# Cross attention of a decoder layer: normalised x written to PSUM, split into fp16 pairs and transposed by DMA, projected in fp16 with a scaled W, in a new instruction order

## What is computed

```python
x = x + attn(layernorm(x))            # one head of 128, scores, softmax, w_o
x = x + xattn(layernorm(x), ctx_1024, mask)
x = x + ffn(layernorm(x))             # ternary weights, 8-bit activations, silu

def xattn(x, y, y_mask):
    x_proj = relu(einsum('bih,oh->bio', x, W) + b)
    y_proj = relu(einsum('bjh,oh->bjo', y, W) + b)
    scores = einsum('bih,bjh->bij', x_proj, y_proj)
    scores = where(y_mask[:, None, :], -inf, scores)
    return einsum('bij,bjh->bih', softmax(scores), y)
```

## Time and profile before

| | us |
|---|---|
| median of 3 runs | 364.05 |
| lowest, highest | 363.34, 364.35 |
| the profiled execution | 364.81 |
| span of its core in the profile | 363.0 |

### The profile page before, as it was taken

The page is one execution under the profiler, slowest core; times in us unless marked ns, Lnnn a source line. Parts: engine busy times, 40 slices in busy tenths (PEclk is TensorE's granted clock), DMA queues, the critical chain, the costliest instruction groups (busy, mean ns, idle before and its releaser), DMA issues.

```text
span 363.0 us, 7155 instructions
## 1 busy us (share of the span) xinstructions
PE 350.5 (97%) x1980; PEld 258.2 (71%) x1980; DVE 323.2 (89%) x932; ACT 311.9 (86%) x583; POOL 293.6 (81%) x421
## 2 busy tenths in 40 slices
PE   8999799999999999999999999999999999999986
PEld 7477578867876767776686776877687667668545
DVE  3689969968899889997899899999999999899994
ACT  3597998999999968999689976899789978898985
POOL 1475859658999998889868998799987897996776
DMA  7984761462046552398456492739564533213353
GB/s 283 419 204 150 173 178 30 124 141 85 17 111 137 118 158 60 79 204 163 88 137 140 66 226 82 159 95 190 116 70 122 114 98 73 46 29 74 93 112 117
DMA packets 84695, 46.09 MB, mean 127 GB/s; under 512 B 76208, under 2 KB 77872, under 8 KB 84272
## 3 DMA queue, kind: packets, MB, share of 16 engines
q1 hardware_dynamic: 84656, 45.64, 52.1%
HBM read 23.07 MB, written 4.21 MB: 75 GB/s over the span
## 4 chain that ended last, share of the span: by engine, by line
PE 52%; DVE 22%; issue 9%; ACT 6%; POOL 6%; DMA 5%; SPq 0%; DVEq 0%; ACTq 0%; POOLq 0%
PE b_bank L1133 6%; PE b_bank L1135 6%; PE b_bank L1134 6%; PE a_bank L1133 3%; PE a_bank L1135 3%; PE a_bank L1134 3%; PE g_bank L1350 3%; PE d_bank L1370 3%; PE u_bank L1350 3%; DMA x_all<-in_x 2%; PE b_bank L1278 2%; DVE h_max L1646 2%; DMA out<-x_all 2%; DVE b_pT_lo L1589 2%; DVE c_work L1619 1%
## 5 line engine op out<-in xcount | busy, mean ns | idle before, releaser
L755 POOL TENSOR_TENSOR c_work<-c_work 128x512 f32<-128x512 f32 x48 | 61.7, 1290 | 5.9 <-DVE c_work L1619 3.6
L1021 ACT ACTIVATE c_work<-g_bank,c_tanh_scale 128x512 f32<-128x512 f32 x52 | 36.2, 696 | 4.5 <-PE g_bank L1350 3.9
L802 POOL TENSOR_SCALAR c_work<-c_work,h_q 128x1024 f32<-128x1024 f32 x28 | 31.5, 1124 | 8.6 <-DVE h_q L1653 8.6
L1133 PE MATMUL b_bank<-ctx_hi,b_pT_hi 128*128 128x256 f32 x128 | 38.2, 299 | 0.1
L1619 DVE SCALAR_TENSOR_TENSOR c_work<-c_work,g_bank 128x512 f32<-128x512 f32 x50 | 33.9, 677 | 3.2 <-ACT c_work L1021 2.8
L1134 PE MATMUL b_bank<-ctx_lo,b_pT_hi 128*128 128x256 f32 x128 | 36.1, 282 | 0.0
L1135 PE MATMUL b_bank<-ctx_hi,b_pT_lo 128*128 128x256 f32 x128 | 36.1, 282 | 0.0
L1350 PE MATMUL g_bank<-gateT,xqT 128*128 128x512 bf16 x112 | 33.6, 382 | 1.3 <-ACT xqT L996 0.7
L1350 PE MATMUL u_bank<-upT,xqT 128*128 128x512 bf16 x112 | 33.6, 381 | 0.3 <-DVE c_work L1614 0.2
L1646 DVE TENSOR_REDUCE h_max<-c_work 128x1 f32<-128x1024 f32 x26 | 31.4, 1209 | 1.0 <-POOL c_work L755 1.0
L1370 PE MATMUL d_bank<-downT,c_half 128*128 128x256 bf16 x240 | 31.2, 273 | 0.2 <-ACT a_xT_raw L1048 0.2
(11 more groups left out here) (375 smaller groups left out, 1237.3 us busy)
## 6 DMA issues: line engine op xcount, KB each, us to landing
ctx_raw<-in_ctx SPq DMA_DIRECT2D x8, 512.0 KB, 4.3
a_xT_raw<-in_x_t SPq DMA_DIRECT2D x7, 512.0 KB, 5.0
ctxT_raw<-in_ctx_t SPq DMA_DIRECT2D x7, 512.0 KB, 4.0
x_all<-in_x SPq DMA_DIRECT2D x7, 512.0 KB, 3.9
out<-x_all SPq DMA_DIRECT2D x7, 512.0 KB, 3.0
r_bc<-r_rows SPq DMA_DIRECT2D x7, 256.0 KB, 4.0
c_work<-in_w_gate SPq DMA_DIRECT2D x1, 1024.0 KB, 9.6
c_work<-in_w_up SPq DMA_DIRECT2D x1, 1024.0 KB, 11.6
```

The source lines that it names most:

```text
L755: pool.tensor_tensor(h[:, t % 2, half * HALF:(half + 1) * HALF], th[:, j % 2, :], up[:, j % 2, :], ALU.mult).then_inc(hs, 1)
L802: pool.tensor_scalar(h_tile(t, n), h_tile(t, n), h_q[:, t:t + 1], ROUND if n < LAST else ROUND_F16, ALU.mult, ALU.add).then_inc(h_rounds, 1)
L1021: act.activation(gate_tile(j, n), gu_bank("g", j, n), ACT.Silu if (n, j) in SILU else ACT.Tanh, scale=c_tanh_scale[:, j // 2:j // 2 + 1]). ...
L1133: pe.matmul(dst, l_hi, r_hi, start=first, stop=False)
```

## The change

1. `b_xn`, `b_T_hi`, `b_T_lo` and the steps XT0 and XT1 on PE are gone. ACT writes the normalised x of a half (two token tiles, 128x512) into a PSUM bank (`b_norm`): `b0`, `b1` for batch 0, `e` for all others. ACT rounds that bank to fp16 (`xn_hi`), DVE subtracts for the low part (`xn_lo`), and SP transposes the pair with one DMA for each half (`transpose_xn`), 128x1024 fp16 each. In the lists these are ACT `B.norm`, ACT and DVE `B.XT0`, `B.XT1`, SP `S.xnT0`, `S.xnT1`.
2. XP0 and XP1 multiply fp16 pairs. W is scaled into the fp16 range once (`w16_max`, a sum over partitions on PE `W.ws`, `w16_scale`, `w16_hi`, `w16_lo`), and the relu takes the scale back (`scale=w16_back`).
3. The `e` bank is shared by YP0, YP1, X0, X1 of all later batches in an order of its own (`E_STEPS`), with the waits that go with it. All five lists are written anew.

```diff
 def b_step(step, n):  # PE
-    if step[:2] == "XT":
...
-            mm = pe.transpose(dst[:, s * P:(s + 1) * P], b_xn[:, s, t * P:(t + 1) * P], ident[:, :])
-    elif step[:2] == "XP":
...
-        pe.wait_ge(b_los, b_lo_rank("XT1", n))
...
+    if step[:2] == "XP":
         if n > 0:
             pe.wait_ge(*o_read(2 + t, n - 1))
...
+        for half in range(2):
+            pe.wait_ge(xn16_loaded[half], 16 * n + 16)
+        xnT = xn16T[:, :, :, :].rearrange("p h (l t c) q -> p h l t c q", l=2, t=2)
         for c in range(DC):
-            mm = product3(dst[:, :], wt_hi[...], wt_lo[...], b_T_hi[:, c, :], b_T_lo[:, c, :], c == 0, c == DC - 1)
+            mm = product3(dst[:, :], w16_hi[...], w16_lo[...], xnT[:, :, 0, :, c, :], xnT[:, :, 1, :, c, :], c == 0, c == DC - 1)
+def b_norm(half, n):  # ACT
+    act.wait_ge(b_shifts, 2 * n + half + 1)
+    before = A_BEFORE[f"X{half}", n]          # who had the bank before
...
+    for i in range(2):
+        t = 2 * half + i
+        last = act.activation(a_bank(f"X{half}", n)[:, i * D:(i + 1) * D], x_tile(n, t), ACT.Identity,
+                              scale=b_rstd[:, t:t + 1], bias=b_shift[:, t:t + 1])
+def xn_hi(half, n):  # ACT
+    act.wait_ge(b_xns, 2 * n + half + 1)
+    if n > 0:
+        act.wait_ge(xn16_loaded[half], 16 * n)
+    act.activation(xn16[:, half, 0:S], a_bank(f"X{half}", n)[:, :], ACT.Copy).then_inc(x_his, 1)
+def xn_lo(half, n):  # DVE
+    dve.wait_ge(x_his, 2 * n + half + 1)
+    dve.tensor_tensor(xn16[:, half, S:2 * S], a_bank(f"X{half}", n)[:, :], xn16[:, half, 0:S], ALU.subtract).then_inc(x_los, 1)
+def transpose_xn(half, n):  # SP
+    sp.wait_ge(x_los, 2 * n + half + 1)
+    if n > 0:
+        sp.wait_ge(xn16_loaded[half], 16 * n)
+        sp.wait_ge(b_filled, b_rank("XP1", n - 1))
+    sp.dma_start(xn16T[:, half], xn16[:, half, :], transpose=True).then_inc(xn16_loaded[half], 16)
+def scale_W(part):  # DVE
...
+        dve.tensor_reduce(w16_max[:, :], W_raw, AX.X, ALU.max, apply_absolute_value=True).then_inc(w16_maxed, 1)
...
+        dve.tensor_scalar(w16_back[:, :], b1_bank[:, 0:1], 1.0e-30, 1.0 / F16_TOP, ALU.max, ALU.mult).then_inc(w16_steps, 1)
...
+        dve.reciprocal(w16_scale[:, :], w16_back[:, :]).then_inc(w16_steps, 1)
...
+        dve.scalar_tensor_tensor(w16_lo[...], W_raw, w16_scale[:, :], w16_hi[...], ALU.mult, ALU.subtract).then_inc(w16_split, 1)
-A_STEPS = "Q K YP0 V VT S0 S1 P0 S2 YP1 P1 S3 P2 P3 H Y0 Y1"
+A_STEPS = "Q K V VT S0 S1 P0 S2 P1 S3 P2 P3 H Y0 Y1"
+X_FIRST = "X0/0 X1/0"
+E_STEPS = """YP0/2 YP1/2 YP0/3 X0/1 X1/1 X0/2 YP1/3 X1/2 YP0/4 YP1/4 X0/3 X1/3 YP0/5 YP1/5 X0/4 X1/4 YP0/6 X0/5
```

More of the change, by code:

```diff
@@ L44 @@
 NEXT_BANKS = ["a0", "a1"]
-E_BANK = "e"
+X_FIRST_BANKS = ["b0", "b1"]
 def a_heir(step, n):
@@ L63, in a_tables @@
     later = [key for key in later if key not in following]
-    turns = [itertools.chain(FRONT_BANKS, itertools.cycle(FRONT_TURN)), iter(SECOND_BANKS), itertools.cycle(NEXT_BANKS)]
+    parts = [front, following, keys(X_FIRST.split()), later, keys(E_STEPS.split())]
+    turns = [itertools.chain(FRONT_BANKS, itertools.cycle(FRONT_TURN)), iter(SECOND_BANKS), iter(X_FIRST_BANKS),
+             itertools.cycle(NEXT_BANKS), itertools.repeat("e")]
     place, banks, before, last = {}, {}, {}, {}
-    for part, turn in zip((front, following, later), turns):
+    for part, turn in zip(parts, turns):
         for step, n in part:
@@ L70, in a_tables @@
             else:
-                if step[:2] != "YP":
+                if step[0] not in "YX" or step[:2] in ("Y0", "Y1"):
                     place[step, n] = len(place)
-                banks[step, n] = E_BANK if part is later and step[:2] == "YP" else next(turn)
+                banks[step, n] = next(turn)
                 before[step, n] = last.get(banks[step, n])
@@ L79 @@
 A_PLACE, A_BANK, A_BEFORE, A_LAST = a_tables()
-B_STEPS = ["XT0", "XT1", "XP0", "XP1", "S0", "S1", "P0", "S2", "P1", "O0", "S3", "P2", "O1", "P3", "O2", "O3"]
+B_STEPS = ["XP0", "XP1", "S0", "S1", "P0", "S2", "P1", "O0", "S3", "P2", "O1", "P3", "O2", "O3"]
 WARM_UP = 6
@@ L85 @@
 DVE_WHOLE = [("K", 0), ("P1", 0), ("P3", 0)]
-B_LO = ["XT0", "XT1", "P0", "P1", "P2", "P3"]
+B_LO = ["P0", "P1", "P2", "P3"]
 NBL = len(B_LO)
@@ L102 @@
 PE_ORDER = """
[L103 to L117, removed]
@@ L118 @@
-    C.g4/3 B.P2/4 B.O1/4 A.H/5 C.g5/3 E.YP0/6 A.Y0/5 A.Y1/5 B.P3/4 C.u5/3 A.Q/6 B.O2/4 C.g6/3 C.u6/3 A.K/6 A.V/6
-    B.O3/4 C.g7/3 B.XT0/5 B.XT1/5 C.u7/3 A.S0/6 C.DN0/3 B.XP0/5 B.XP1/5 C.u0/4 C.g0/4 E.YP1/6 A.S1/6 A.S2/6
-    C.DN1/3 C.u1/4 C.g1/4 B.S0/5 B.S1/5 C.DN2/3 C.g2/4 A.S3/6 C.DN3/3 C.u2/4 B.P0/5 B.S2/5 B.P1/5 C.u3/4 C.g3/4
-    B.O0/5 B.S3/5 C.g4/4 C.u4/4 B.P2/5 B.O1/5 A.H/6 C.u5/4 B.P3/5 C.g5/4 C.u6/4 A.Y0/6 A.Y1/6 B.O2/5 A.Q/7 A.K/7
-    B.O3/5 A.V/7 A.S0/7 C.g6/4 B.XT0/6 B.XT1/6 C.DN0/4 C.u7/4 C.g7/4 A.S1/7 B.XP0/6 B.XP1/6 C.g0/5 E.YP0/7
@@ L1079, in step @@
                     if stream == "B":
[L1080 to L1084 removed]
+                        b_norm(half, n)
                     else:
@@ L1394, in step @@
                     mm.then_inc(v_sums, 1)
+                elif name == "ws":
+                    pe.wait_ge(w16_maxed, 1)
+                    pe.wait_ge(v_steps, 1)
+                    pe.matmul(b1_bank[:, 0:1], ones[:, :], w16_max[:, :], start=True, stop=True).then_inc(w16_summed, 1)
                 elif name == "total":
+                    pe.wait_ge(w16_steps, 1)
                     pe.wait_ge(v_steps, 1)
```

346 lines of the change are left out of this document (193 added, 153 removed).

## The result

The change makes the kernel slower: 374.72 us median of 4 runs (373.77 to 378.69) against 364.02 (363.34 to 364.35), ratio 1.0317 with an interval of 1.0239 to 1.0395. The prediction said 359.7 us and faster, with a range of 355.0 to 365.0. The profiled execution took 378.69 us with a span of 376.6, against 364.81 and 363.0; it is the slowest of the four, so what is read from its trace explains 13.6 us of span and not the 10.7 us between the medians.

The account below looks back on a forecast made before the run. PE was taken as the bound by a little, DVE next. 363.0 - 8.8 (PE's work) + 0.2 (sum for W's scale) + 2.4 (batch 0) + 1.9 (DVE) = 358.7 us span, 359.7 us predicted; range 355.0 to 365.0.

Parts of the forecast that it names:

- What bounds the kernel: Whole kernel, chiefly 100 to 340 us: PE is full and the bound by a little, DVE next at 94.2%.
- PE's own work, -8.8 us: PE: 7.3 us from removed transposes of x and 1.5 us from shorter fp16 matmuls of XP0 and XP1.
- The fall of PE's busy time by 17 us: Sign on the profile page: PE's busy time down by some 17 us of records, 8.7 of XT among them.
- ACT and DVE at nothing: Normalisations, roundings and subtractions of x: same counts with fp16 out, 0.3 us more over two engines, taken at nothing.
- Scaled W, hidden: Preparation of W: 2 us of DVE in steps of about 0.7 us or less, hidden in idle time before 40 us.
- Batch 0, +2.4 us, XP0 at 50.6: Batch 0: DMA path not covered, 1.17 us of transposes not gained and XP0 1.2 us later, +2.4 us.
- the last part: Closing list of signs: prediction wrong if batch 0's delay grows along the pipeline, or POOL or ACT turns out next.
- The DMA wait, covered in batches 1 to 7: Before XP0: other PE work covers the transposes' latency; tightest batch 5 some 0.6 us short, bounds 0 to 1.5 a batch.
- DVE gives back 1.9: 100 to 340 us: DVE holds 96%, not the needed 96.8%, +1.9 us, bounds 0 and +6.4.
- Rival 2 (SP's queue), 372 us: SP: transposes of x held 5.8 us behind others stop PE 1.8 us or more a batch, 12.6 in all; chance 0.14.
- Rival 1 (PE's work brings nothing): 100 to 340 us: DVE at 94.2% is the bound, so PE's 6.4 us do not come; 364 us, chance 0.15.

Follow-up runs that it names:

- x_oneXT: Kernel before, with one PE transpose instead of four in each of XT0 and XT1 of batches 1 to 7: 365.52 us, ratio 1.0027.
- x_lessACT: Kernel before, batches 1 to 7: one PE transpose of four, DVE's subtraction and ACT's rounding of x over 64 of 512 columns: 364.28 us, ratio 1.0000.
- x_front: Changed kernel with two entries of DVE's list moved, A.ag1/1 earlier and W.wl/0 later: 373.34 us, ratio 1.0277.
- x_nowait: Changed kernel, XP0 and XP1 of batches 1 to 7 multiply a fixed buffer without waiting for the transposes, which are still issued: 371.93 us, ratio 1.0216.
- x_free: Changed kernel, batches 1 to 7: XP does not wait for the transposes, and these take a constant source without waiting for x: 369.49 us, ratio 1.0180.
- x_late: Kernel before, with XP0 of each batch waiting for one added small store of 128x4 numbers on SP: 389.54 us, ratio 1.0656.
- x_bslot: Kernel before without the loads of x of batches 4 to 7, which use the output of four batches before: 364.06 us, ratio 0.9994.
- x_slot: Changed kernel without the loads of x of batches 4 to 7, which use the output of four batches before: 372.23 us, ratio 1.0238.

## Why the prediction was wrong, step by step

- **What bounds the kernel: wrong, and the root of the error.** "PE is not waiting, it is full" was read from distances inside groups of matmuls; it is true there and says nothing of what happens when a group gets shorter. PE's list then reaches the next step earlier and waits for other streams. `x_oneXT` to `x_lessACT` measure it: 4.6 us on PE, 6 on DVE, 4 on ACT, sum zero.
- **PE's own work, -8.8 us: right** (8.5 by the starts; fp16 matmuls of XP at 0.214 us for 0.217), but it is no gain. The fall of PE's busy time by 17 us that I named as a sign was mis-sized: it was 4.6. The rows give only 8.7 us of XT and some 2 us of XP (records of 0.38 for 0.40 us), and the rest has no working.
- **ACT and DVE at nothing: right for what was counted, and one term was left out.** The normalisation, the rounding and the subtraction cost 0.564, 0.595 and 0.684 us. The relu with the scale costs 0.79 us for 0.705, 2.6 us of ACT. What it costs in time no run measures.
- **Scaled W, hidden: wrong.** `w_lo` took 2.22 us where I said 0.7 or less, and stood on the chain to XP0 of batch 0, in DVE's list ahead of the second shift. Away from a long POOL instruction it takes 0.78 us (last section), so the price was nearly right and the place was wrong. `x_front`, which moves it, is 1.4 us faster by the medians, inside the intervals.
- **Batch 0, +2.4 us, XP0 at 50.6: mis-sized.** It began at 53.5, 4.2 us later than before instead of 1.2. The normalisations started 1.4 us later than I had them (45.45), and the four took 3.8 us for 2.07, since the second pair waited for the shift behind `w_lo`; the landing was as priced (2.76). The delay grew along the pipeline, which the last part named as the way to be wrong.
- **The DMA wait, covered in batches 1 to 7: wrong.** The landing was priced rightly (2.8 us median against 3.0 to 3.5 assumed; three of batches 4 and 5 took 4.2 to 4.5, and one of batch 6 took 5.1). The path before it was not: I counted 2.07 us for four normalisations, and the second half came 2.6 to 3.8 us behind the first in batches 3 to 6 and 5.9 in batch 7, for it needs the `e` bank and has other entries ahead of it. From the first normalisation to XP0 batches 3 to 7 took 9.4 to 12.9 us, where I had 6.9. PE's waits on `xn16T` were 5.7 us, of which batch 0 has 1.7.
- **DVE gives back 1.9: wrong.** DVE did not rise to 96% from 100 us on but fell to 90%.
- **Rival 2 (SP's queue), 372 us: nearest in time, not in mechanism.** Its sign was there (more than 3 us of waits outside batch 0), and the queue did hold transposes that had their data, by 0.4 to 2.0 us in five places, never by 5.8; `x_nowait` and `x_free` give 5.2 us for wait and queue together, half of the loss, and it was to be 12.6.
- **Rival 1 (PE's work brings nothing): right in the effect, wrong in the cause.** Less work on PE is worth nothing, but DVE is not the bound. Its 364 us left out what the new waits cost.
- **Missed altogether:** that added latency at XP0 is paid at least in full (`x_late`: 18.7 us of waits, 25 us of time, with the lower clock and SP's queue in the difference), that the new lists bring 5 us of delay in the first 131 us with or without the transposes, and, by the medians, that the change loads loops that had slack, as the one through the slots of x (`x_bslot` 0, `x_slot` 2.5 us).

The loss of 10.7 us in parts, by medians: 5.2 the transposes of batches 1 to 7 with wait, queue and traffic, up to 1.4 the two entries in the front, up to 2.5 the loop; together 6.5. The rest, over 4 us, lies in the new lists, the dearer relu and the longer path that is left without the DMA, and by the traces ahead of 131 us; which entries hold it is open.

## What to carry to other kernels

In a kernel whose engines take hand-laid lists in order, a full engine is no proof of a bound: before counting work taken away as a gain, take a part of it away alone and measure, and add a microsecond of pure latency at the place as the second test. If less work brings nothing and more latency costs in full, as at XP0 here, judge a change by when its data arrive at each list, not by what it saves. A path through another queue has to be timed from its first input to its last landing, with the entries between its steps, in every batch.
